# Cross phase of a decoder layer: output projection in three split passes, gate columns side by side, residual loaded by tile

## The reference, cut to what matters

```python
x = _layernorm(x + self_attention(x, ...))                     # self and memory phases
v, k, q = (per head: ctx @ Wv.T, ctx @ Wk.T, x @ Wq.T)
attention = softmax(einsum('nqhd,nkhd->nhqk', q, k) / sqrt(512))
out = einsum('nhql,nlhd->nqhd', attention, v).reshape(N, Lq, EMBED)
x = _layernorm(x + (out @ Wo.T + bo))                          # the projection in question
logits = einsum('bsd,de->bse', tokens, gate_w)                 # 512 -> 8 experts
weights = softmax(logits); topk_w, topk_idx = top_k(weights, 2)
out = silu(x @ w0.T + b0) * fw[:, 0:1] * m0 + silu(x @ w1.T + b1) * fw[:, 1:2] * m1
x = _layernorm(x + out)
```

## Time and profile before

| what | value |
|---|---|
| median of 3 runs | 1813.93 us (1813.42 to 1819.52) |
| the profiled execution | 1817.17 us, span 1815.4 us, mean granted clock 0.974 |
| PE busy | 1729.1 us (95%) |
| DVE busy | 1266.5 us (70%) |
| POOL busy | 1133.6 us (62%) |
| ACT busy | 963.2 us (53%) |
| one batch of the cross phase | 106.3 us |

### The profile page before, as it was taken

How to read it: one execution, slowest core, us unless ns; L and a number is a source line. 1 busy time by engine, 2 the same in 40 slices (tenths; PEclk the granted TensorE clock), 3 DMA queues, 4 the chain that set the end, 5 groups by cost and what they waited for, 6 DMA issues and landing times.

```text
span 1815.4 us, 30316 instructions
## 1 busy us (share of the span) xinstructions
PE 1729.1 (95%) x10474; PEld 1092.8 (60%) x10474; DVE 1266.5 (70%) x2792; ACT 963.2 (53%) x1895; POOL 1133.6 (62%) x933
## 2 busy tenths in 40 slices
PE   5999999999999989999988899999999999999997
PEld 4666666666666557887753346465554646555456
DVE  5677777777777657777857586767768677776744
ACT  3555555555555532433345466555656555565554
POOL 2556556565564544655457776777687686768773
PEclk9999999999999869999988899999999999999999
DMA  6555555565554464676625544344434434443200
GB/s 195 143 146 164 141 155 167 140 164 147 153 157 123 118 205 130 195 213 182 180 91 137 124 111 134 89 110 122 106 100 112 124 88 122 122 102 93 74 26 24
DMA packets 166884, 237.24 MB, mean 131 GB/s; under 512 B 21702, under 2 KB 72902, under 8 KB 166732
## 3 DMA queue, kind: packets, MB, share of 16 engines
q1 hardware_dynamic: 166732, 235.31, 46.8%
HBM read 91.57 MB, written 41.94 MB: 74 GB/s over the span
## 4 chain that ended last, share of the span: by engine, by line
PE 69%; POOL 9%; DVE 8%; DMA 4%; issue 4%; ACT 3%; SPq 3%; POOLq 0%; ACTq 0%; DVEq 0%
PE bank L201 8%; PE bank L1553 8%; PE bank L202 6%; PE bank L203 6%; POOL cross_added L1846 5%; PE bank L351 5%; PE bank L296 4%; PE bank L1376 4%; PE bank L1437 4%; PE bank L1405 4%; PE bank L338 4%; PE bank L1504 2%; SPq L684 2%; DVE cross_negmax L1386 2%; PE bank L316 2%
## 5 line engine op out<-in xcount | busy, mean ns | idle before, releaser
L1386 DVE TENSOR_REDUCE cross_negmax<-bank 128x1 f32<-128x512 f32 x512 | 339.5, 676 | 167.6 <-PE bank L1376 163.1
L1623 ACT ACTIVATE cpt<-bank 128x512 f32<-128x512 f32 x512 | 295.9, 595 | 160.9 <-PE bank L1405 153.9
L525 DVE CUSTOM_DVE_ANT_0 bank<-bank,future 128x128 f32<-128x128 f32 (+3 forms) x512 | 246.8, 488 | 173.4 <-PE bank L338 172.7
L410 ACT ACTIVATE pt<-bank 128x256 f32<-128x256 f32 (+3 forms) x512 | 224.2, 440 | 257.2 <-PE bank L296 256.2
L1846 POOL TENSOR_TENSOR cross_added<-cross_added,cpt 128x2048 f32<-128x2048 f32 x64 | 292.3, 4567 | 27.4 <-ACT cpt L1623 26.7
L1376 PE MATMUL bank<-cqk 96*128 96x512 f32 x512 | 254.9, 501 | 20.4 <-DMA cqk<-cstage 9.4
L1405 PE MATMUL bank<-cqk 98*128 98x512 f32 x512 | 227.7, 445 | 12.0 <-ACT cpt L1623 11.0
L589 POOL TENSOR_SCALAR_AFFINE_SELECT pt<-pt 128x512 f32<-128x512 f32 x128 | 81.3, 635 | 252.2 <-ACT pt L410 252.2
L1846 POOL TENSOR_TENSOR cross_added<-cpt,cpt 128x2048 f32<-128x2048 f32 x32 | 146.5, 4577 | 107.0 <-ACT cpt L1623 107.0
L201 PE MATMUL bank<-xt_hi,w_hi 128*128 128x512 f32 x384 | 169.2, 441 | 17.3 <-DVE w_lo L483 14.2
L296 PE MATMUL bank<-qk 98*128 98x256 f32 (+2 forms) x512 | 181.5, 358 | 3.5 <-DMA qk<-self_shift 2.3
(11 more groups left out here) (199 smaller groups left out, 3549.9 us busy)
## 6 DMA issues: line engine op xcount, KB each, us to landing
qk<-stage SPq DMA_DIRECT2D x384, 128.0 KB, 2.4
cqk<-cstage SPq DMA_DIRECT2D x384, 128.0 KB, 2.3
scratch_memory<-memory SPq DMA_DIRECT2D x32, 512.0 KB, 3.8
ma<-scratch_memory SPq DMA_DIRECT2D x32, 512.0 KB, 4.0
raw<-in_x_t SPq DMA_DIRECT2D x32, 256.0 KB, 2.8
v<-in_x SPq DMA_DIRECT2D x32, 256.0 KB, 3.2
scratch_y_ar<-y_ar SPq DMA_DIRECT2D x32, 256.0 KB, 2.2
my_ar<-scratch_y_ar SPq DMA_DIRECT2D x32, 256.0 KB, 4.5
```

Source lines behind the costliest of these rows:

```text
L410: act.activation(s.pt[step % 3][:, j, 0:SEQ - first], sh.bank[2 + n % 2][:, first - q0:SEQ - q0], ACT.Exp, scale=SCALE_SELF).then_inc(s.ac ...
L525: dve.tensor_tensor_reduce(out=scores, in0=scores, in1=sh.future[:, SEQ - P * (qt + 1):SEQ], scale=-1.0, scalar=-NEG, op0=ALU.add, op1=ALU ...
L1386: dve.reduce_max(s.negmax[gm % 2][:, col:col + 1], max_bank(sh, m)[:, :], AX, negate=True).then_inc(s.dve_max, 1)
L1623: act.activation(s.pt[step % 3][:, j, :], sh.bank[2 + n % 2][:, :], ACT.Exp, scale=SCALE_CROSS).then_inc(s.act_exp, 1)
```

## The change

In the cross phase:

- **Projection.** Each fp32 chunk becomes three fp32r passes: y_hi·wo_hi, y_hi·wo_lo, y_lo·wo_hi. For this ACT splits wo (slots 33, 37, 43, 47, once) and DVE subtracts its low parts one slot later; each group ACT copies y_hi at slot 12 and DVE subtracts y_lo at slot 13. The multiplication of slot 9 is written in place into y_raw.
- **Gate.** The high and low columns of the gate stand side by side, so that a chunk takes two passes of 16 columns instead of three of 8. Eight small fp32 products then add the high and low logits and transpose them, in the place of four transposes.
- **Residual.** x1 is loaded by tile, at positions 6, 12, 18 and 24, straight into x2, after the store that used the tile; the last batch's go to x3. The second norm works in place.
- **Stacks.** The landing semaphores count by head, and PE's maxima wait for their own head's quarter.
- **Buffers.** The x1 groups have two buffers instead of three; some semaphores are shared with the self phase.

At the start: the bias loads stand behind the K weights, and the high part of x's fifth tile behind the K2 weights' high parts on ACT.

The core of the diff:

```diff
-        done = pe.matmul(bank[:, :], s.y[:, (GROUPS * b + c) % (GROUPS + 1), tile_of(k)], cw.wo[:, c, :], start=False, stop=(c == GROUPS - 1))
+        if k == 0:
+            pe.wait_ge(s.dve_y, GROUPS * b + c + 1)
+        done = cross_project(pe, s, bank, k, c)
...
+def cross_project(pe, s, bank, k, c):
+    hi, lo = s.y_hi[:, c, tile_of(k)], s.y_lo[c][:, tile_of(k)]
+    pe.matmul(bank[:, :], hi, s.wo_hi[:, c, :], start=False, stop=False)
+    pe.matmul(bank[:, :], hi, s.wo_lo[:, c, :], start=False, stop=False)
+    return pe.matmul(bank[:, :], lo, s.wo_hi[:, c, :], start=False, stop=(c == GROUPS - 1))
...
 def cross_slot_scalar(act, second, s, cw, sh, n):
+    if at == 12 and 0 <= g - 1 < NG:
+        e = g - 1
+        act.wait_ge(s.dve_norm, (TILES + 1) * (e + 1))
+        if e >= GROUPS:
+            act.wait_ge(s.pe_po, TILES * (e // GROUPS))
+        act.activation(s.y_hi[:, e % GROUPS, :], s.y_raw[:, :], ACT.Copy).then_inc(s.act_y, 1)
...
 def cross_slot_vector(dve, s, cw, sh, n):
-        dve.tensor_tensor(s.y[:, e % (GROUPS + 1), :], sh.bank[5][:, :], s.y_raw[:, :], ALU.mult).then_inc(s.dve_norm, 1)
+        dve.tensor_tensor(s.y_raw[:, :], sh.bank[5][:, :], s.y_raw[:, :], ALU.mult).then_inc(s.dve_norm, 1)
+    if at == 13 and 0 <= g - 1 < NG:
+        e = g - 1
+        dve.wait_ge(s.act_y, e + 1)
+        dve.tensor_tensor(s.y_lo[e % GROUPS][:, :], s.y_raw[:, :], s.y_hi[:, e % GROUPS, :].bitcast(F32),
+                          ALU.subtract).then_inc(s.dve_y, 1)
+    if n - 1 in SPLIT_WO:
+        c = SPLIT_WO.index(n - 1)
+        dve.wait_ge(s.act_wo, c + 1)
+        dve.tensor_tensor(s.wo_lo[:, c, :], cw.wo[:, c, :], s.wo_hi[:, c, :].bitcast(F32), ALU.subtract).then_inc(cw.dve_small, 1)
...
 def cross_max(pe, s, sh, m):
-        pe.wait_ge(s.kq_landed[gm % 3], 48 * PER * (gm // 3 + 1))
+    if qt == 0:
+        stack_landed(pe, s, gm, jm)
...
-        done = triple(pe, sh.bank[6][0:EXPERTS, :], (cw.gate_hi[:, c, :], cw.gate_lo[:, c, :]),
-                      (s.x2t_hi[:, c, :], s.x2t_lo[:, c, :]), c == 0, c == GROUPS - 1)
+        logits = sh.bank[6][0:2 * EXPERTS, :]
+        pe.matmul(logits, cw.gate[:, c, :], s.x2t_hi[:, c, :], start=(c == 0), stop=False)
+        done = pe.matmul(logits, cw.gate[:, c, :], s.x2t_lo[:, c, :], start=False, stop=(c == GROUPS - 1))
...
+            for part in range(2):
+                done = pe.matmul(sh.bank[7][:, k * EXPERTS:(k + 1) * EXPERTS], s.x1t[0:2 * EXPERTS, tile_of(k)],
+                                 sh.ident[0:2 * EXPERTS, EXPERTS * part:EXPERTS * part + EXPERTS],
+                                 start=(part == 0), stop=(part == 1))
...
+LOAD_X1 = (6, 12, 18, 24)
...
+    if 0 <= b < LAST_BATCH and n % BATCH_SLOTS in LOAD_X1:
+        k = LOAD_X1.index(n % BATCH_SLOTS)
...
+            sp.wait_ge(s.out_stored[k % 2], 16 * (2 * b - 1 + k // 2))
+        cross_load_x1(sp, second, s, b, k, s.x2)
...
-        if i == GROUPS - 1:
-            sp.dma_start(s.bias[:, 0:2 * GROUPS], t["b_attn"]).then_inc(s.w_landed[0], 16)
-            sp.dma_start(s.bias[:, 2 * GROUPS:], t["b_k2"]).then_inc(s.w_landed[0], 16)
+        if i == 2 * GROUPS - 1:
+            sp.dma_start(s.bias[:, 0:2 * GROUPS], t["b_attn"]).then_inc(s.w_landed[1], 16)
+            sp.dma_start(s.bias[:, 2 * GROUPS:], t["b_k2"]).then_inc(s.w_landed[1], 16)
```

More of the change, by code:

```diff
@@ L457, in self_scalar, with self_x_high @@
                            scale=-RELU).then_inc(s.act_q, 1)
[L458 to L464, removed]
-    arrive(act, sh.self_done)
+        if kt == 3 and j == 3 and GROUPS < g + 7 < NG:
+            self_x_high(act, s, g + 7)
+    arrive(act, sh.self_done)
+def self_x_high(act, s, x):
+    b, c = divmod(x, GROUPS)
+    act.wait_ge(s.raw_landed[c], 16 * (b + 1))
+    if b >= 2:
+        act.wait_ge(s.pe_k2, GROUPS * (b - 1))
+    act.activation(s.xt_hi[b % 2][:, c, :], s.raw[c][:, :], ACT.Copy).then_inc(s.act_xt, 1)
 def self_weight(s, i):
@@ L703, in __init__ @@
         self.a = sb("a", [P, P])
-        self.gate_hi, self.gate_lo = (sb(f"gate_{part}", [P, GROUPS, EXPERTS], F32R) for part in ("hi", "lo"))
+        self.gate = sb("gate", [P, GROUPS, 2 * EXPERTS], F32R)
         self.gate_raw = sb("gate_raw", [P, GROUPS, EXPERTS])
@@ L945, in memory_project, with memory_scalar @@
     done.then_inc(s.pe_po, 1)
-def memory_scalar(act, s, third, sh):
+def memory_scalar(act, s, third, cw, sh):
     for i in MEMORY_ROUNDS:
@@ L1262, with __init__ @@
 class CrossPhase:
-    def __init__(self, nc, ctx, t, second, weights_end):
+    def __init__(self, nc, ctx, t, first, second, weights_end):
         def sem(name):
@@ L1271, in __init__ @@
         self.stage = sb("cstage", [P, 4, SEQ])
-        self.x1g = [sb(f"x1_group{i}", [P, TILES, P]) for i in range(3)]
+        self.x1g = [sb(f"x1_group{i}", [P, TILES, P]) for i in range(2)]
+        y_low = [sb("cy_lo0", [P, SEQ], F32R)]
         self.x1t = sb("x1t", [P, SEQ])
@@ L1327, in __init__ @@
         self.dve_gate, self.act_exp_hi, self.pool_exp_lo = sem("dve_gate"), sem("act_experts"), sem("pool_experts")
-        self.weight_landed = [sem(f"expert_landed{i}") for i in range(2)]
+        self.weight_landed = first.w_landed
 LAST_BATCH = BATCH - 1
@@ L1900, in cross_slot_sync @@
     b = n // BATCH_SLOTS - 1
[L1901 removed]
+    if 0 <= b < LAST_BATCH and n % BATCH_SLOTS in LOAD_X1:
+        k = LOAD_X1.index(n % BATCH_SLOTS)
+        if b == 0 and k == 0:
+            sp.wait_ge(sh.memory_done, 4)
         if b >= 1:
[L1903 to L1907 removed]
+            sp.wait_ge(s.out_stored[k % 2], 16 * (2 * b - 1 + k // 2))
+        cross_load_x1(sp, second, s, b, k, s.x2)
+    if n == NS + 1:
+        sp.wait_ge(s.pe_st, NS - SLOTS)
+        sp.wait_ge(s.pe_mx, NS)
+        for k in range(TILES):
+            cross_load_x1(sp, second, s, LAST_BATCH, k, s.x3)
     for b, slot in behind(n):
@@ L1923, in cross_load_keys @@
     if d >= 1:
-        sp.wait_ge(s.kq_landed[(d - 1) % 3], 48 * PER * ((d - 1) // 3 + 1))
+        for j in range(PER):
+            stack_landed(sp, s, d - 1, j)
     sp.dma_start(s.stage[:, 3, :], s.t["ctx_t"][b, tile_of(h), :]).then_inc(s.keys_landed, 16)
@@ L1976, in tail_project @@
             cross_bias(pe, cw, sh.bank[k], 0)
-        pe.wait_ge(s.dve_norm, (TILES + 1) * (GROUPS * b + c + 1))
-        done = pe.matmul(sh.bank[k][:, :], s.y[:, (GROUPS * b + c) % (GROUPS + 1), tile_of(k)], cw.wo[:, c, :],
-                         start=False, stop=(c == GROUPS - 1))
+        pe.wait_ge(s.dve_y, GROUPS * b + c + 1)
+        done = cross_project(pe, s, sh.bank[k], k, c)
         if c == GROUPS - 1:
@@ L2129, in build @@
         second = MemoryPhase(nc, place, sems, t)
-        third = CrossPhase(nc, sems, t, second, weights_end)
+        third = CrossPhase(nc, sems, t, first, second, weights_end)
         with nc.Block() as block:
@@ L2140, in _ @@
                 self_scalar(act, first, second, third, sh)
-                memory_scalar(act, second, third, sh)
-                cross_scalar(act, second, third, sh)
+                memory_scalar(act, second, third, cw, sh)
+                cross_scalar(act, second, third, cw, sh)
             @block.vector
```

121 lines of the change are left out of this document (64 added, 57 removed).

## The result

| | median us | runs, us |
|---|---|---|
| before | 1816.72 | 1813.42 to 1820.06, 4 runs |
| after | 1839.28 | 1836.49 to 1844.31, 4 runs |

The change makes the kernel slower: ratio 1.0127, 95% interval 1.0094 to 1.0160. The forecast was 1830 within 1802 to 1845, slower by about 15 us; the medians differ by 22.6 us, the two profiled executions (1836.49 and 1817.17) by 19.3.

A forecast was written before the change was run, and what follows sets the result against it. PE is busy 95%, but POOL and DVE bound parts of each cross batch. Terms −0.9 − 1.7 + 16.0 + 0.9 − 1.65 = +12.65, plus 2.3 for the clock, took 1816.0 to 1831; forecast 1830, range 1802 to 1845.

The forecast's parts named there:

- the upper end: Cross phase, y_lo's subtraction: DVE waits to the end of the running POOL add, up to 4.57 us, rather than 0.9.
- Projection, −0.96: Cross batch: three fp32r passes save 0.16 us a chunk, but only six chunks at positions 15 to 20 count: −0.96.
- Position 13, +0.48: Cross batch, position 13: y_lo's subtraction holds POOL's factors to about 0.48 us later, on the POOL path.
- Position 29, +1.2: Cross batch, position 29: y_lo waits for POOL's add, delaying statistics, POOL's factors and all POOL work up to the totals: +1.2 us.
- Gate and logits: Cross batch, positions 38 to 41: passes save 0.93 us of PE, small matmuls cost +0.6 to +1.4; DVE-bound, so nothing.
- Position 45, +1.95: Cross batch, position 45: y_lo waits for POOL's add and the maximum PE needs two slots on comes late: +1.95 us.
- The clock term: Cross batches: PE idle of some 2 us at position 45 may lower the clock, 1.17 us each, two of six: +2.3.
- Start and first groups: Start: moved bias loads give −0.9 us. First cross groups: waits by head −7.7, split of wo and y_lo +6: −1.7.
- Hidden subtraction (1800): Rival: in the cross batches y_lo's subtraction slips in or its lateness stays within slack, all gains stay: 1800 us; chance 0.14.
- The full cut (1779): Rival: PE's whole cut, 37 us from projection, gate, tail, start and waits, reaches the end: 1779 us; chance 0.02.
- Half absorbed (1814 to 1818): Rival: DVE let in early at positions 29 and 45, about 1814 us, or half the waits, 1818; chance 0.17.
- All waits full and the clock down in each batch (1840): Rival: clock costs +7 and wo's split +10: 1840 us, with a late tile 3 up to 1845; chance 0.05.

The follow-up runs named there:

- bank input: Changed kernel, but y_lo's subtraction takes its first input from the PSUM bank of the maximum DVE reduces next: 1816.21 us.
- the subtraction alone: Kernel before plus one DVE subtraction at slot 13 in 29 groups: 1853.58 us with two SBUF inputs, 1822.84 us with a PSUM bank as one.
- the fp32 projection: Changed kernel with the projection in fp32 as before, without the splits of y and wo: 1817.10 us.
- the logits back in time: Changed kernel with gate in twelve passes and four transposes as before, y_lo's subtraction still on two SBUF inputs: 1848.43 us.
- loads and waits alone: Changed kernel with projection, gate and logits as before; only first loads, residual by tile, waits by head and buffers changed: 1805.73 us.
- wo on POOL: Changed kernel with gate and logits as before, y split from its PSUM bank, and wo's subtractions moved from DVE to POOL: 1802.51 us.
- the one with two identities: Changed kernel with y split from its PSUM bank, and logits by four fp32 matmuls against two stacked identities instead of eight: 1824.89 us.

## Why the prediction was right

**The mechanism** was read rightly off two pairs of rows of the memory phase: the end of the subtraction follows the end of the POOL operation. The choice of the upper end, the whole add, held: 2.78 at position 29, up to 4.69. The bank input (−23 us against the changed kernel) and the pair with the subtraction alone (+37 against +6) show it. The traces show the shutting out up to a POOL add of 4.58 us, behind which a subtraction of wo took 4.58 and one of y_lo 4.69, and in both directions: POOL's factors took 0.54 for 0.22.

**The sum of a batch** was +2.67 without the clock; the five steady batches are longer by 2.75 to 5.16. That the lowest of them come so near is luck. No batch of after is without a stretch at the lower clock, and most have two, where I had counted two falls in six batches, apart from the sum. In the batch of the table, term by term:
- Projection, −0.96: −1.1 to −1.5 between positions 16 and 28. The twelve chunks there gave about 0.1 each; I had let those from position 20 on give nothing. (At 12 to 14 lie three chunks, not four.)
- Position 13, +0.48: +0.2 at position 16 in the two batches in which the clock stays up there, +0.33 with the subtraction alone. The +0.5 of the table has a fall of the clock in it.
- Position 29, +1.2 through POOL and the totals at 36: +2.3, and it came sooner, at the maximum of position 31. With the bank as input the same place costs +0.9, so the shut-out itself is 1.4. I had followed the statistics to POOL and not the maximum behind them to PE, which has only two slots.
- Gate and logits, "nothing, since DVE is the bound": wrong in both halves. By the run with the fp32 projection the passes give −0.9 and the logits cost +1.8 up to position 44. An engine that is the bound can be starved by the one that feeds it, if that one is late by more than the lead: DVE stood idle for 1.34 us there.
- Position 45, +1.95: nothing. PE doesn't wait behind it; the late logits let the add run out. The +1.0 between positions 44 and 48 is the clock's: the run with the fp32 projection, which has no such subtraction, loses 1.1 to 2.0 there where the clock falls and nothing where it doesn't. With the logits back in time the same place costs +2.1, and with the fall of the clock behind it 1.9 more. So my price was about right for the kernel without the logits' delay.
- Position 61, nothing: right, though the subtraction takes 2.78 there.

So the late logits and the clock, neither of which I had in the sum of a batch, stood in for the price of position 45. The clock term, +2.3 for two falls, was too small. No run shows its premise, that an idle PE brings a fall: the changed kernel has one of 3.41 us behind the logits in each of six batches, and PE has no gap ahead of the one at 1300.5.

**The signs.** Four came: the mean of y_lo, 2.18 us; the batches, 109.1 to 111.7 for 108 to 110; the waits of the maxima for stacks, of which none is left; and the tail's projection, 0.69 a chunk. Two did not, and both belong to the paths that I had wrong: the totals wait for POOL for 0.3 us in all (3.4 before), not for over 1 us each, and PE's maxima behind position 45 don't wait for DVE.

**Start and first groups.** The start gave −2.1, beyond the range −0.3 to −1.5. The step that failed was that the biases held back ACT's first weights. They are gone from that wait, but the weights themselves land no sooner:

```profile
10.02 2.19 ACT L482 ACTIVATE w_hi<-pt 128x512 fp32r<-128x512 f32 x4 [2.59 <-DMA pt<-in_w_attn_t]
```

This is 0.12 sooner than in the earlier trace rows, and so was the first matmul (11.63 for 11.75). But with the high part of x's fifth tile moved behind the K2 weights, PE's next products started at 22.10 for 22.62, and the stack's first scores waited 3.39 for 3.85 and began at 41.04 for 42.17. The last 1.0 of the gain is the clock's, at the lower level for 3.41 us there and for 6.83 before. In the two runs that leave the start as it was, the self phase's first scores come at 52.81 and 53.53 for 51.38, so one trace doesn't settle the size. The −1.8 between start and cross phase isn't explained by the change; PE's clock was at the lower level there for 37.6 us instead of 47.8, and in the other traces this stretch differs from before by −5.6 to +1.8.

The first cross groups gave −0.2 for −1.7; with the fp32 projection the same slots give −10.2 and with loads and waits alone −9.2, so the gain of the waits was larger than counted and the price of the split of wo, 6, too small, near the upper bound of 10. These sizes are rough: the two runs with the subtraction alone, which leave stacks and wo as they were, show −3.1 and −0.7 in these slots.

**The last pass and the tail.** +3.4 for +0.9: I had said that DVE has less to do there. But position 29 cost +4.0 up to position 36, with the clock down for 6.83 us from position 31 on, and the logits cost +1.5; behind position 44, with no fall of the clock, nothing was lost. The tail gave −1.1 within its bounds.

**The rivals.** Hidden subtraction (1800): fell, although a kernel with a free subtraction does come out at 1802.5, with the gate as before and wo on POOL. The full cut (1779): fell. Half absorbed (1814 to 1818): fell in the whole, but at position 45 hardly a wait was left. All waits full and the clock down in each batch (1840): the time came nearest to this, and the half on the clock came true, with 0.95 to 0.98 granted in the batches for 0.98 to 1.00.

## What to carry to other kernels

Before a vector operation is added, ask where its inputs lie and what POOL does at that moment: 0.69 us with a PSUM bank as one input, up to 4.7 with both in SBUF beside a POOL add. Where two delays stand in a row, the sum isn't a sum: removing the earlier one can send the later one into a worse collision, so such changes are tested together. And saving passes on an engine that feeds the bound helps only if the small operations that then stand on the path, here sixteen records of 0.11 us, don't take it back. Before a loss is put down to a wait, see what the granted clock did in that stretch: here about 1 us a batch was the clock's and looked like the subtraction's.

## What the runs showed of the hardware

The shutting out works both ways: POOL instructions that begin while DVE subtracts from two SBUF inputs are held as well (0.22 became 0.54, 1.28 became 1.72). A waiting instruction counts as busy in the profile (a y_lo subtraction 2.18 us on the mean, 0.68 at its shortest), so DVE's busy time rose by 71 us where some 25 are work. And a fp32 matmul of 16x8 leaves two records at 0.11 us from start to start, so sixteen take 1.95 us at a granted clock of 1.00, nearly five times the 0.41 of the four transposes that they replace. Behind these small records, positions 43 to 46, the granted clock fell to the lower level, 0.50 for 3.41 us and more, in all six batches of the changed kernel and of the one with two identities, in four of six with the fp32 projection and in three of six with the bank input; with four transposes it fell there in none, in seven kernels. That the small records bring the fall about is not shown.
